# Attention: where GpSimd makes the low parts of the output weights and of the key-value weights

## What is computed

```python
q = (x @ Wq.T).reshape(b, t, N_HEADS, HEAD_DIM).transpose(0, 2, 1, 3)
k = (x @ Wk.T).reshape(b, t, N_KV_HEADS, HEAD_DIM).transpose(0, 2, 1, 3)
v = (x @ Wv.T).reshape(b, t, N_KV_HEADS, HEAD_DIM).transpose(0, 2, 1, 3)
q = _qknorm(q, q_scale)
k = _qknorm(k, k_scale)
...
scores = jnp.einsum('bhtd,bhsd->bhts', q, k) * scale
scores = jnp.where(causal, scores, jnp.finfo(scores.dtype).min)
attn = jax.nn.softmax(scores, axis=-1)
out = jnp.einsum('bhts,bhsd->bhtd', attn, v)
return out @ Wo.T
```

## Time and profile before

| | us |
|---|---|
| median of three runs | 915.0 |
| lowest and highest of the three | 912.89, 915.06 |
| profiled execution, device time | 913.11 |
| its span in the trace | 911.3 |
| PE busy | 888.7 (98%) |
| DVE busy | 539.4 (59%) |
| ACT busy | 430.2 (47%) |
| POOL busy | 318.1 (35%) |

### The profile page before, as it was taken

The page is one execution under the profiler, slowest core; times in us unless marked ns, Lnnn a source line. Parts: engine busy times, 40 slices in busy tenths (PEclk is TensorE's granted clock), DMA queues, the critical chain, the costliest instruction groups (busy, mean ns, idle before and its releaser), DMA issues. The chain is left out here.

```text
span 911.3 us, 16964 instructions
## 1 busy us (share of the span) xinstructions
PE 888.7 (98%) x5696; PEld 778.5 (85%) x5701; DVE 539.4 (59%) x1361; ACT 430.2 (47%) x948; POOL 318.1 (35%) x286
## 2 busy tenths in 40 slices
PE   9999999999999997999999999999999999999998
PEld 7999768888888885789978988897887888888887
DVE  5999996333333336688578668867876533333333
ACT  3522345433343333577466657646654443343433
POOL 5111022555655553221221212122102455555563
PEclk9999999999999999999999999999999999999999
DMA  8999211111111102000100000000001111111111
GB/s 341 339 370 396 95 37 45 37 52 52 35 52 52 52 18 96 0 25 1 36 23 0 35 0 23 0 0 0 1 1 35 37 52 52 52 35 52 52 42 55
DMA packets 25952, 60.98 MB, mean 67 GB/s; under 512 B 3314, under 2 KB 11188, under 8 KB 25908
## 3 DMA queue, kind: packets, MB, share of 16 engines
q1 hardware_dynamic: 23604, 47.82, 15.6%
q0 software_dynamic: 2304, 12.58, 3.7%
HBM read 59.35 MB, written 1.05 MB: 66 GB/s over the span
## 5 line engine op out<-in xcount | busy, mean ns | idle before, releaser
L863 DVE TENSOR_TENSOR f_h<-f_scaled,bank 128x512 f32<-128x512 f32 (+1 forms) x90 | 60.9, 676 | 183.6 <-POOL f_scaled L760 183.6
L760 POOL TENSOR_TENSOR f_scaled<-f_act,f_gate_rows 128x512 f32<-128x512 f32 (+1 forms) x90 | 113.6, 1263 | 133.1 <-ACT f_act L685 132.8
L953 PE MATMUL bank<-f_xt_hi,f_w_hi 128*128 128x512 f32 (+2 forms) x400 | 157.1, 393 | 1.0 <-ACT f_xt_hi L137 0.5
L953 PE MATMUL bank<-f_xt_hi,f_w_lo 128*128 128x512 f32 (+2 forms) x400 | 157.1, 393 | 0.0
L692 ACT ACTIVATE f_h_hi<-f_h 128x512 fp32r<-128x512 f32 (+2 forms) x102 | 63.6, 624 | 187.0 <-DVE f_h L863 187.0
L953 PE MATMUL bank<-f_xt_lo,f_w_hi 128*128 128x512 f32 (+2 forms) x400 | 124.6, 392 | 0.7 <-DVE f_xt_lo L112 0.5
L1128 ACT ACTIVATE at_prob<-bank,at_sbias,at_qrs 128x512 f32<-128x512 f32 (+3 forms) x128 | 77.6, 617 | 85.5 <-DVE at_sbias L1304 85.5
L970 PE MATMUL bank<-f_w_lo,f_h_hi 128*128 128x256 f32 (+1 forms) x400 | 113.2, 283 | 0.0
L970 PE MATMUL bank<-f_w_hi,f_h_lo 128*128 128x256 f32 (+1 forms) x400 | 113.2, 283 | 0.0
L970 PE MATMUL bank<-f_w_hi,f_h_hi 128*128 128x256 f32 (+1 forms) x400 | 113.1, 283 | 0.0
L872 DVE TENSOR_TENSOR f_h_lo<-f_h,f_h_hi 128x512 fp32r<-128x512 f32 (+2 forms) x102 | 70.2, 688 | 71.9 <-ACT f_h_hi L692 71.6
(11 more groups left out here) (179 smaller groups left out, 2023.7 us busy)
## 6 DMA issues: line engine op xcount, KB each, us to landing
cv_raw<-in_wconv SPq DMA_DIRECT2D x26, 512.0 KB, 6.4
cv_shared<-in_wtaps POOLq DMA_DIRECT2D x16, 768.0 KB, 7.4
f_wraw<-in_w SPq DMA_DIRECT2D x44, 256.0 KB, 2.7
xn<-in_wconv SPq DMA_DIRECT2D x14, 512.0 KB, 6.2
f_wraw<-in_w SPq DMA_DIRECT2D x44, 128.0 KB, 2.5
at_wraw<-in_wqkv SPq DMA_DIRECT2D x3, 768.0 KB, 4.3
at_oraw<-in_wo SPq DMA_DIRECT2D x4, 512.0 KB, 3.6
X<-in_x_tiles SPq DMA_DIRECT2D x2, 512.0 KB, 7.9
```

The source lines that it names most:

```text
L760: g.tensor_tensor(scaled[half][:, cols], act[half][:, cols], gate_rows[:, half * HALF + cols.start:half * HALF + cols.stop], ALU.mult).the ...
L863: v.tensor_tensor(h_f[half][0:rows, cols], src[half][0:rows, cols], pu[half][0:rows, cols], ALU.mult)\
L953: mm = t.matmul(bank[half][0:out_rows, :], w, x, start=q == 0, stop=q == len(steps) - 1)
```

## The change

POOL's `at_wo_lo` is now two instructions of half the columns each (128x512). Both move: the first stands between the powers of units 2 and 3 behind a wait for `at_prob_done` of unit 2, the second between the powers of units 3 and 4 behind a wait for that of unit 3. `at_wkv_lo` of the next group moves from directly behind the power of unit 4 to just ahead of that of unit 5, behind a wait for `at_prob_done` of unit 4. `at_wo_lo_done` now counts two for each group, which changes the numbers in three waits (SP's and PE's), not their places.

```diff
-                sp.wait_ge(s["wo_lo_done"], g)
+                sp.wait_ge(s["wo_lo_done"], g * 2)
                 sp.dma_start(oraw[:], ins["wo"][bass.ds(g, 1)].rearrange("a p f -> (a p) f")).then_inc(s["o_in"], 16)
...
+            def behind_probabilities(g, u):
+
+                p.wait_ge(s["prob_done"], g * NU * NQ + NQ * (u + 1))
+
+            def low_output_weights(g, part):
+                p.wait_ge(s["wo_hi_done"], g + 1)
+                heads = slice(part * REP // 2, (part + 1) * REP // 2)
+                cols = slice(heads.start * D, heads.stop * D)
+                p.tensor_tensor(wo_lo[:, heads, :].rearrange("p h d -> p (h d)"), oraw[:, cols],
+                                wo_hi[:, heads, :].rearrange("p h d -> p (h d)").bitcast(F32), ALU.subtract)\
+                 .then_inc(s["wo_lo_done"], 1)
+
             def group(g, last):
                 for u in range(1, NU):
+                    if u in (3, 4):
+                        behind_probabilities(g, u - 1)
+                        low_output_weights(g, u - 3)
+                    if u == 5 and not last:
+                        behind_probabilities(g, u - 1)
+                        low_kv_weights(g + 1)
                     query_factor(g, u)
-                    if u == 2:
-                        p.wait_ge(s["wo_hi_done"], g + 1)
-                        p.tensor_tensor(wo_lo[:].rearrange("p h d -> p (h d)"), oraw[:],
-                                        wo_hi[:].rearrange("p h d -> p (h d)").bitcast(F32), ALU.subtract)\
-                         .then_inc(s["wo_lo_done"], 1)
-                    if u == 4 and not last:
-                        low_kv_weights(g + 1)
...
-                        t.wait_ge(s["wo_lo_done"], g + 1)
+                        t.wait_ge(s["wo_lo_done"], g * 2 + 2)
```

## The result

| | before | after |
|---|---|---|
| median, six runs each, us | 913.93 | 909.31 |
| lowest and highest, us | 912.63, 915.06 | 907.47, 910.2 |
| span of the profiled execution, us | 911.3 | 905.7 |

The ratio is 0.995, with a 95% interval from 0.9938 to 0.9962: 3.5 to 5.7 us faster. The forecast was 909.1.

The account below looks back on a forecast made before the run. PE was taken as the bound, delayed in step 2 by at_sbias held under POOL's at_wo_lo; removing 1.25 us (once) and 1.24 (three times) gives 4.97, other parts nothing, so 914.1 becomes 909.1, range 907.2 to 911.2.

Parts of the forecast that it names:

- What is bound, and by what: Step 2: DVE's at_sbias is held until POOL's at_wo_lo subtraction of SBUF tiles ends, delaying PE; excess 4.97 us.
- The sum, 4.97 us: Excess of the four at_sbias holds in step 2, 5.61 less 0.64 us, all expected to reach the end.
- taking the hold out of step 2: Moving all of at_wo_lo out of step 2 starts step 3 1.25 us earlier per group; 4.97 us in all.
- the first half: Half of at_wo_lo behind the scaling of unit 2: 1.28 us on POOL, beside PSUM-reading DVE work, cost zero.
- moving the key-value weights: at_wkv_lo one step later frees step 4's at_sbias of 0.16 us in three groups; counted nothing, at most 0.5.
- The new places: POOL slots behind the scalings of units 2, 3 and 4, claimed free: DVE's PSUM-reading instructions there are not held.
- the far bound: First half priced at a whole at_wo_lo, 2.40 us: unit 3's first exponential 0.4 late, cost still about zero.
- PE reads its results only in step 4: Reason given why unit 3's first exponential coming 0.4 us late would cost about zero.
- The waits left to PE: PE's value block in step 2: first of two waits for DVE gone, second about 0.15 to 0.45 us.
- (a): Rival: the hold goes but little reaches the end; if half were lost, 2.5 us gain, 911.6; chance 0.06.
- (b): Rival: no change, the long at_sbias isn't POOL's doing or the hold reappears elsewhere; 914.1; chance 0.04.
- (c): Rival: DVE subtractions reading one SBUF input are held too at the new places; 6.5 us slower, 920.6; chance 0.03.

Follow-up runs that it names:

- the fills: Kernel before, with POOL's low-output-weights subtraction at the old place replaced by one tiny subtraction and two fills, weights left zero; 908.09 against 913.54 (0.994).

## Why the prediction was right

**What is bound, and by what.** Right. The hold ends with the POOL instruction (the split alone lets `at_sbias` in at the seam), and in step 2 its cost follows its length. It is not POOL's being busy (a fill of 2.66 us holds nothing), and `at_sbias` made of two one-tensor instructions is not held (0.21 and 0.20). That two SBUF tensors are needed is not shown, and for wider instructions it is wrong: the 128x128 scaling has one and is held.

**The sum, 4.97 us.** The stretch gave 5.05 (1.26, 1.24, 1.24 and 1.25 in the four steps 2), and the ratio's interval of 3.5 to 5.7 us holds both. Step 2 was to last 8.4 and lasts 8.37. Of the four edits' terms: taking the hold out of step 2 is the whole gain; the first half costs nothing at its new place, the second neither; moving the key-value weights is worth at most 0.12 us, which neither a time nor the stretch can tell from nothing.

**The new places.** Right in the result, with small errors in the working. I gave the semaphore 0.07 us; the first half started 0.17 behind the scaling in group 0. The power of unit 3 then started 0.14 behind `at_qsum`, where I had allowed 0.1 at most; the slack took it. SP's load of the next output weights starts at 399.44 instead of 388.52, 11 us later and not 13, since I left out the shift. And I called the far bound, a power delayed by a whole 2.40 us, "still about zero": with the whole instruction moved the stretch was 0.88 us longer, some 0.55 of it in step 3. The step that failed there was "PE reads its results only in step 4": in that kernel the `at_sbias` of unit 3 waits 0.54 us for the late power, `at_qt_lo` stands behind it in DVE's order and ends at 399.88, and PE's next scores start at 400.02, 0.15 late.

**The waits left to PE.** I expected 0.15 to 0.45 us at the second wait of the value block, and 0.24 is there.

**The rivals.** (a) fell: the shift passed whole. (b) fell: no `at_sbias` is held anywhere. (c), the slower one, had the right mechanism on the wrong instruction. The PSUM-reading subtractions are not held, but the scaling is, and had the wait stood 0.2 us earlier the change would have been slower than before, by 4.4 us in the stretch. I had the scaling in view only as the event behind which POOL starts, and did not price its being late. The list of what to check did name longer scaling tiles.

**The level of before.** I took 914.1 as the middle of two pairs 2 us apart, and the six runs of before had a median of 913.93. That the forecast of 909.1 came within 0.2 of the measured 909.31 is luck in part: both samples happened to split three and three, so both medians are middles between two levels. Level against level the gain is 4.7 and 4.8 us (the means of the lower three, 912.80 and 908.12, and of the upper three, 915.01 and 910.17), and 5.05 in the stretch. The two levels are the matter of the last section.

## What to carry to other kernels

A tiny instruction whose maximum is nine times its median, and whose end agrees each time with the end of an instruction on another engine, was being held here: subtract the median, follow the chain to the bound engine, and check that PE's own work doesn't become the limit first. Where GpSimd must read SBUF, give it a slot in which VectorE works from PSUM, and check every VectorE instruction in the slot, the wide SBUF-to-SBUF ones as well as those with two tensors; if no slot is wide enough, cut the GpSimd instruction, as a seam alone brought nine tenths of the gain here, where it happened to come 0.27 us behind the start of the held instruction. Moving work one step does not by itself help: the same hold in a steady step still cost 0.97 of its 1.27 us.

## What the runs showed of the hardware that was not expected

**Two levels of the time.** The runs of most kernels fell into two groups about 1.5 to 2 us apart. The group goes with PE's mean granted clock: of the 43 executions of the kernel before whose clock is on record, the 30 up to 913.62 us have 0.999 or 1.000, the 13 from 914.79 us on have 0.997 or 0.998, and none lies between. The place is visible where a profile caught one of the lower clock. Of the fourteen profiles, the five with a mean clock of 0.998 or less all have a fall at the start of the attention, and none of the nine others has one there. PE's busy time and granted clock at the start of the attention, first in the kernel with only the key-value weights moved (mean clock 0.997), then in the changed kernel (1.000); the columns are the stretch, its length, PE's busy time and matmuls, the granted clock, the share of the DMA engines and GB/s:

```profile
350.00:355.00 5.00, 1.93 (x12) 0.95 0.46 121
355.00:360.00 5.00, 5.00 (x32) 0.71 0.51 163
```

```profile
350.00:355.00 5.00, 2.64 (x21) 1.00 0.62 172
355.00:360.00 5.00, 3.43 (x30) 1.00 0.49 150
```

In the first the clock is at its lower level, 1.2 of 2.4 GHz, for some 3 us, and two neighbouring matmuls there, from the timeline of the same kernel, start 0.21 apart; at the full clock those of this form start 0.12 apart:

```profile
354.78 0.56 PE L1400 MATMUL bank<-at_wkv_hi,at_xt_hi 128*128 128x256 f32 x1 [2.37 <-DVE at_xt_lo L112]
...
355.35 0.41 PE L1400 MATMUL bank<-at_wkv_lo,at_xt_hi 128*128 128x256 f32 x1
355.56 0.41 PE L1400 MATMUL bank<-at_wkv_hi,at_xt_hi 128*128 128x256 f32 x1
...
358.15 0.28 PE L1400 MATMUL bank<-at_wkv_hi,at_xt_lo 128*128 128x256 f32 x1
358.27 0.28 PE L1400 MATMUL bank<-at_wkv_lo,at_xt_hi 128*128 128x256 f32 x1
```

Just ahead of it, PE waits 2.4 us for `at_xt_lo`. Two kernels change only this hole.

```diff
-        xt_hi, xt_lo, xt_hi_done, xt_done, ln = layernorm_engines("at", factors, ps[4:8], 3, ctx, nc, cm, pm, ps)
+        xt_hi, xt_lo, xt_hi_done, xt_done, ln = layernorm_engines("at", factors, ps[4:8], 12, ctx, nc, cm, pm, ps)
```

> The changed kernel with 12 in place of 3 filler matmuls behind the first transposes of the attention, where PE idles for 2.4 us. In the profiles of four kernels the granted clock fell to half for about 3 us just behind this place, and their first scores come 1.3 to 1.6 us later. Theory: the fall comes after this idle time in some executions and makes the upper of the two levels that the runs of every kernel show; with the hole filled it doesn't come, all runs lie on the lower level, 907.5 to 908.5. Rival (the two levels have another cause, for example the loads at the start): the same spread as before, 907.5 to 910.2.

Measured: 907.94 (907.77 to 908.44) against 912.95 (0.9945, 0.9928 to 0.9962); all four executions have a clock of 1.000. (Of the four kernels that the expectation speaks of, the traces taken by then show the fall in three.) With the fillers the hole in front of the first products is 0.43 us.

The second has 0 in the place of the 3:

> The opposite of the kernel with more fillers: the changed kernel without the 3 filler matmuls in PE's hole at the start of the attention, which makes the hole some 0.7 us longer (3.0 in place of 2.4 us). The fillers are on no path, so without an effect on the clock the runs lie as those of the changed kernel: some at 907.5 to 908.5 with a granted clock of 1.000, about a third to a half at 910.1 with 0.998. If the hole is what brings the clock down, the share of executions at the upper level grows, to nearly all, median 910.1.

Measured: 909.88 (909.76 to 911.22) against 913.44 (0.9961, 0.9946 to 0.9976); all five executions have a clock of 0.995 to 0.998. The hole is 3.01 us, in the timeline:

```profile
355.03 0.35 PE L1406 MATMUL bank<-at_wkv_hi,at_xt_hi 128*128 128x256 f32 x1 [3.01 <-DVE at_xt_lo L112]
```

and behind it the stretch reads:

```profile
355.00:360.00 5.00, 4.97 (x29) 0.66 0.51 166
```

So with a hole of 3.0 us five of five executions lost clock, with 2.4 us three of six of the changed kernel, with 0.4 us none of four. The last count says little by itself: three other kernels with the hole of 2.4 us (the whole instruction moved, the first half in place, the fills) have none of four either. Over all kernels with that hole 35 of 98 executions have a clock of 0.998 or less, against none of the eight with fillers, the kernel below counted in. At 35 of 98, five of five would come up in about 0.6% of cases and none of eight in about 3%, if executions are independent of one another; that is an estimate from these counts. So with the longer hole the fall is more frequent; that filling the hole prevents it is likely, not shown. Where the clock does not fall the execution is 1.5 to 2 us shorter. Nine more fillers don't make the kernel's fastest execution faster (907.77 against 907.47); none of their four lies at the upper level. Both last changes together:

> The fillers and the other order of DVE in step 2 together. If they add up: 907.0 on one level.

Measured: 907.56 (906.6 to 907.84) against 912.95 (0.9936, 0.9918 to 0.9954), the stretch 307.77, as with the other order alone (307.76). The four executions lie at 0.999 or 1.000. The median is 0.4 below that of the kernel with fillers alone and no lower than that of the kernel with the other order alone (907.49); the 907.0 expected did not come, and these times don't show that the two add up.

**A second fall of the clock.** In the kernel that waits for the exponentials PE idled 1.11 us at the end of step 2 of group 0, and the next step ran with a granted clock of 0.81:

```profile
385.00:394.60 9.60, 8.13 (x53) 6.74 (x53) 8.41 (x23) 8.32 (x21) 2.46 (x2) 1.00 0.00 0
394.60:403.80 9.20, 9.18 (x52) 8.05 (x52) 7.45 (x18) 5.29 (x15) 2.29 (x2) 0.81 0.09 11
```

The columns are the stretch, its length, busy time and instructions of PE, PEld, DVE, ACT and POOL, then the granted clock. That step took 9.22 us, and 8.24 and 8.25 in groups 1 and 2: one more microsecond, in one group of four. That the hole brought the clock down is argued, not shown: PE idled 1.10, 1.10 and 1.03 us at the same place of the other three groups, and their clock stayed. What decides whether it comes is open.
